# A four-layer sequence kernel: VectorE computes y first at the changes of unit, and the experts' weights and six norms are prepared in the mixer's last steps

## The reference

```
# mixer: 128 heads of 64 channels, 8 groups, state of 128; four-tap causal convolution on x, B, C
gate, xBC, dt = split(x @ in_proj_w.T);  xBC = silu(conv(xBC) + conv_b)
y = ssd(x_heads, -exp(A_log), B, C, D, softplus(dt + dt_bias))    # in chunks, with a carried state
g = y * silu(gate);  g = g * rsqrt(mean(g*g over a group's 1024 channels) + eps) * norm_w
x3 = layernorm(x2 + g @ out_w.T)
# experts: 28 of them, the two best per token
base = x3 @ base_W.T;  logits = x3 @ gate_W.T;  h = x3 @ lora_A.T (28 x 8 columns)
out = layernorm(x3 + base + (h * gates * 2) @ lora_B)
```

## Time and profile before

| | |
|---|---|
| time, median of 3 runs | 2229.35 us |
| profiled execution: time | 2232.77 us |
| profiled execution: span of instructions | 2230.7 us |
| busy: PE / PEld / DVE / ACT / POOL | 2085.4 / 1627.8 / 1717.7 / 1444.4 / 1144.1 us |
| mean granted clock of TensorE, share of full | 0.974 |

### The profile page before, as it was taken

One profiled execution on the slowest core, in us unless ns is written; L12 is line 12 of the kernel. 1 busy time (PEld: TensorE's weight loads), 2 busy tenths in 40 slices (PEclk: granted clock), 3 DMA queues, 4 the chain that ended last, 5 costly groups with the idle time before them and its releaser, 6 DMA issues. The chain is left out here.

```text
span 2230.7 us, 32403 instructions
## 1 busy us (share of the span) xinstructions
PE 2085.4 (93%) x10968; PEld 1627.8 (73%) x10968; DVE 1717.7 (77%) x2864; ACT 1444.4 (65%) x2823; POOL 1144.1 (51%) x976
## 2 busy tenths in 40 slices
PE   8899896999999999999999999999999999999968
PEld 4666575787777778777877777778777777777755
DVE  4777574878887988788778877887888788878766
ACT  1566524776777676767776778667767776777631
POOL 3554240555555564565465646564656465545531
PEclk9899997999999999999999999999999999999979
DMA  4000011312131213221322122112221212121111
GB/s 161 1 0 0 1 53 40 94 64 86 39 99 62 84 46 92 81 73 39 99 71 72 63 75 71 71 63 76 70 76 58 80 67 86 48 86 57 38 37 38
DMA packets 72194, 140.28 MB, mean 63 GB/s; under 512 B 34449, under 2 KB 35473, under 8 KB 67826
## 3 DMA queue, kind: packets, MB, share of 16 engines
q1 hardware_dynamic: 72050, 138.44, 18.6%
HBM read 134.74 MB, written 3.67 MB: 62 GB/s over the span
## 5 line engine op out<-in xcount | busy, mean ns | idle before, releaser
L92 PE MATMUL p_out<-w_out,yT 128*128 128x512 f32 x1536 | 384.4, 400 | 22.2 <-issue 14.2
L92 PE MATMUL p_mix<-x_high,w_x 128*128 128x512 f32 x1024 | 384.2, 437 | 1.4 <-DVE x_low L1028 1.4
L1680 POOL TENSOR_TENSOR wq_t<-wq_t,cb 128x1024 f32<-128x1024 f32 x128 | 326.7, 2552 | 88.2 <-DVE cb L1555 85.5
L92 PEld LDWEIGHTS p_out<-w_out,yT 128*128 128x128 f32 x1536 | 291.9, 192 | 90.9 <-issue 18.2
L764 DVE SCALAR_TENSOR_TENSOR conv<-p_mix,unit_small,conv 128x511 f32<-128x511 f32 (+2 forms) x384 | 287.0, 747 | 89.2 <-ACT conv L744 80.1
L92 PE MATMUL p_gate<-w_gate,x_high 128*128 128x512 f32 x1024 | 327.5, 401 | 0.2 <-ACT silu_gate L1406 0.2
L1398 ACT ACTIVATE wq_t<-wq_t,minus_cum 128x128 f32<-128x128 f32 x1024 | 313.9, 389 | 1.4
L1335 PEld LDWEIGHTS p_intra<-x_dt,wq_t 128*128 128x128 f32 x2048 | 241.0, 192 | 4.6 <-POOL wq_t L1680 2.2
L1335 PE MATMUL p_intra<-x_dt,wq_t 128*128 128x64 f32 x2048 | 242.8, 272 | 1.0 <-POOL wq_t L1680 1.0
L92 PEld LDWEIGHTS p_mix<-x_high,w_x 128*128 128x128 f32 x1024 | 195.3, 191 | 62.5 <-issue 22.2
L752 ACT ACTIVATE x_channels<-conv 128x512 f32<-128x512 f32 x128 | 80.8, 631 | 222.1 <-DVE conv L764 220.5
(11 more groups left out here) (228 smaller groups left out, 4248.3 us busy)
## 6 DMA issues: line engine op xcount, KB each, us to landing
cum_all<-cum_rows SPq DMA_DIRECT2D x128, 512.0 KB, 3.6
w_staged<-in_w_gate SPq DMA_DIRECT2D x16, 1024.0 KB, 6.0
w_raw_tiles<-in_w_x SPq DMA_DIRECT2D x64, 256.0 KB, 3.7
w_staged<-in_w_out SPq DMA_DIRECT2D x16, 1024.0 KB, 4.8
w_raw_tiles<-in_w_bc SPq DMA_DIRECT2D x16, 256.0 KB, 2.7
x<-in_x SPq DMA_DIRECT2D x1, 2048.0 KB, 17.4
out<-z SPq DMA_DIRECT2D x8, 256.0 KB, 2.0
wqkv<-in_wqkv SPq DMA_DIRECT2D x4, 384.0 KB, 5.4
```

What stands on the lines that cost most here:

```text
L92: last = pe.matmul(dst, left[a](k), right[b](k), start=k == 0 and n_ == 0, stop=stop and k == tiles - 1 and n_ == 2)
L1680: pool.tensor_tensor(decay[:, k % 2], decay[:, k % 2], cb[:, c].unsqueeze(1).to_broadcast([P, UNIT_HEADS, P]), ALU.mult).then_inc(decay_do ...
```

## The change

In the mixer VectorE's order is another one at the changes of unit. `make_y` is the old code of y. In the last step of a unit it stands ahead of the taps; in the first, all four low parts of `w_out` stand ahead of it and the output sum behind it. The output sum of step 14 goes to step 0 of the next group, `arguments` of step 1 and 9 behind the copies of `p_mix`, and the cast and low part of `w_bc` from step 8 to step 9 on both engines.

A class `Ahead` holds what the last group does for the experts. Their weights go to buffers of the mixer that are free by then: raw tiles to `w_staged`, `w_raw_tiles` and `conv`, loaded in step 13; high and low parts to `w_x`, `w_bc` and, for the last low part, `w_gate`; `w_lora_b` to `cum_all`, loaded in step 15. ScalarE makes the high parts at the ends of steps 14 and 15, GpSimd all four low parts there. In steps 12 to 15 VectorE takes the moments of chunks 0 and 1, 2 and 3, 4, and 5 behind y, and the norm of the chunk before; GpSimd takes their powers behind `inv_rms`. In the experts the loads, splits and first six moments fall away; `pS` lies in `p_mix`.

```diff
+class Ahead:
...
+    NORMED = {2 * CHUNKS - 4: (0, 1), 2 * CHUNKS - 3: (2, 3), 2 * CHUNKS - 2: (4,), 2 * CHUNKS - 1: (5,)}
+    def high_part(self, act, k):
+        act.wait_ge(self.in_w4[k], 16)
+        act.activation(self.high[k], self.raw[k], ACT.Copy).then_inc(self.w4_high, 1)
+    def low_part(self, pool, k, gate_done):
+        pool.wait_ge(self.w4_high, k + 1)
+        if k == KT - 1:
+            pool.wait_ge(gate_done, GROUPS * STEPS)
+        pool.tensor_tensor(self.low[k], self.raw[k], self.high[k].bitcast(F32), ALU.subtract).then_inc(self.w4_low, 1)
+    def moments(self, dve, i, src):
+        dve.bn_stats(self.stats[:, i % 2], src).then_inc(self.stats_done, 1)
+        dve.wait_ge(self.stats_done, 2 * i + 1)
+        dve.bn_aggr(self.mv[:, i], self.stats[:, i % 2]).then_inc(self.stats_done, 1)
+        dve.wait_ge(self.stats_done, 2 * i + 2)
+        dve.tensor_scalar(self.mv[:, i, 1:2], self.mv[:, i, 1:2], EPS, None, ALU.add).then_inc(self.var_done, 1)
+    def inverse(self, pool, i, neg_half):
+        pool.wait_ge(self.var_done, i + 1)
+        pool.tensor_tensor(self.rstd[:, i:i + 1], self.mv[:, i, 1:2], neg_half, ALU.pow).then_inc(self.rstd_done, 1)
+    def norm(self, dve, i, dst, sem):
+        dve.wait_ge(self.rstd_done, i + 1)
+        dve.tensor_scalar(dst, dst, self.mv[:, i, 0:1], self.rstd[:, i:i + 1], ALU.subtract, ALU.mult).then_inc(sem, 1)
...
@@ mixer, SP
+                        if last and k == 2 * CHUNKS - 3:
+                            sp.wait_ge(out_split, 2 * GROUPS * UT)
+                            sp.wait_ge(front.x_w_split, 2 * GROUPS * UT)
+                            sp.wait_ge(conv_done, PLAN.ready(g, CHUNKS + CPS - 1, ("x", UT - 1, 1)))
+                            ahead.load_weights(sp, d["w_experts"])
+                        if last and k == 2 * CHUNKS - 1:
+                            sp.wait_ge(arg_done, GROUPS * STEPS)
+                            ahead.load_lora(sp, d["w_lora_b"])
@@ mixer, ScalarE: high_part(0), (1) at the end of step 14; (2), (3) in step 15 behind the square
@@ mixer, VectorE
+                def ahead_norm(k):
+                    for i in ahead.NORMED[k]:
+                        dve.wait_ge(both_done, (GROUPS - 1) * CHUNKS + i + 1)
+                        ahead.moments(dve, i, acc[:, i])
+                        if i:
+                            ahead.norm(dve, i - 1, acc[:, i - 1], ahead.norm3)
-                        early = c > 0 and k + 1 < STEPS
-                        if early:
+                        if c > 1 and k + 1 < STEPS:
                             arguments(s + 1, k + 1)
...
+                        if c == 1:
+                            arguments(s + 1, k + 1)
...
                             y_low_part(*before)
+                        if k == 0 and not first:
+                            out_sum(g - 1, STEPS - 2)
...
+                        if c == CHUNKS - 1:
+                            make_y(g, k)
+                            taps_of(events)
+                            if last and half:
+                                ahead_norm(k)
+                            continue
+                        taps_of(events)
+                        if summed and c:
                             out_sum(*before)
...
-                        if k == CHUNKS and not last:
+                        if k == CHUNKS + 1 and not last:
                             for j in range(2):
                                 front.bc_high_part(dve, g * 5 + 6, j)
                         if c == 0:
-                            out_low_part(g * 2 + half, half, (0, 1))
+                            out_low_part(g * 2 + half, half)
...
+                        make_y(g, k)
+                        if summed and c == 0:
                             out_sum(*before)
-                        if c == 0:
-                            out_low_part(g * 2 + half, half, (2, 3))
+                        if last and k >= 2 * CHUNKS - 4:
+                            ahead_norm(k)
@@ mixer, GpSimd
                             inverse_rms(*before)
+                        if last and k >= 2 * CHUNKS - 4:
+                            for i in ahead.NORMED[k]:
+                                ahead.inverse(pool, i, neg_half[:])
+                        if last and k >= 2 * CHUNKS - 2:
+                            for i in range(2):
+                                ahead.low_part(pool, (k - 2 * CHUNKS + 2) * 2 + i, gate_done)
...
-                        if k == CHUNKS and not last:
+                        if k == CHUNKS + 1 and not last:
@@ experts, VectorE
-                for c in range(CHUNKS):
-                    moments(c, x3[:, c])
-                    if c:
-                        norm(c - 1, x3[:, c - 1], norm3)
...
+                for c in range(EARLY, CHUNKS):
+                    ahead.moments(dve, c, x3[:, c])
+                    ahead.norm(dve, c - 1, x3[:, c - 1], norm3)
+                    if c == EARLY:
+                        low(0)
+                ahead.norm(dve, CHUNKS - 1, x3[:, CHUNKS - 1], norm3)
```

More of the change, by code:

```diff
@@ L1457, in group @@
                         if c == CHUNKS - 1:
+                            if half and last:
+                                ahead.high_part(act, 2)
+                                ahead.high_part(act, 3)
                             if half and not last:
@@ L1470, in group @@
                             empty_x(g, k + 1)
+                        if last and k == 2 * CHUNKS - 2:
+                            ahead.high_part(act, 0)
+                            ahead.high_part(act, 1)
                 groups(act, group)
@@ L1478, in _, with out_low_part @@
                 dve.memset(neg_half[:], -0.5).then_inc(const3, 1)
-                def out_low_part(unit, half, tiles):
-                    for j in tiles:
+                def out_low_part(unit, half):
+                    for j in range(UT):
                         at_ = UT * (TAPS + 1) + j
@@ L1535, in out_sum, with make_y @@
                                              ALU.mult, ALU.add).then_inc(both_done, 1)
+                def make_y(g, k):
+                    s, c = step(g, k), k % CHUNKS
+                    dve.wait_ge(intra_done, s + 1)
+                    if carries(c):
+                        dve.wait_ge(skip_sum, n_carries(g, k) + 1)
+                    else:
+                        dve.wait_ge(xskip_done, s + 1)
+                    yk = y[:, k % 2]
+                    wait(dve, sq_done, s - 1)
+                    dve.tensor_tensor(yk, p_intra[:], xskip[:].rearrange("p h e -> p (h e)"),
+                                      ALU.add).then_inc(y_sum, 1)
+                    dve.wait_ge(sg_done, s + 1)
+                    dve.wait_ge(y_sum, s + 1)
+                    dve.tensor_tensor(yk, yk, sg[:], ALU.mult).then_inc(y_done, 1)
+                def ahead_norm(k):
[4 more added lines that the diff above has]
+                            ahead.norm(dve, i - 1, acc[:, i - 1], ahead.norm3)
                 def group(g, first, last):
@@ L1707, in experts @@
         n = Named(nc, ctx)
-        ident, x3 = keep["ident"], keep["acc"]
-        w = n.sb("w_experts", [P, KT, DIM + SIDE])
-        w_high = n.sb("w_experts_high", [P, KT, DIM + SIDE], F32R)
-        w_low = n.sb("w_experts_low", [P, KT, DIM + SIDE], F32R)
-        wb = n.sb("w_lora_b", [P, 2, DIM])
+        ident, x3, ahead = keep["ident"], keep["acc"], keep["ahead"]
+        w_high, w_low, wb = ahead.high, ahead.low, ahead.lora
         iota = n.sb("iota", [P, EXPERTS])
         neg_half = n.sb("neg_half4", [P, 1])
-        stats = n.sb("ln4_stats", [P, 2, nc.vector.BN_STATS_DIM])
-        mv = n.sb("ln4_mv", [P, 2 * CHUNKS, 2])
-        ve = n.sb("ln4_ve", [P, 2 * CHUNKS])
-        rstd = n.sb("ln4_rstd", [P, 2 * CHUNKS])
         xT = n.sb("x3T", [P, 2, 2, KT, P], F32R)
@@ L1807, in _ @@
                 flip(0)
-                pe.wait_ge(w4_low, 2)
-                pe.wait_ge(w4_low_pool, 2)
+                pe.wait_ge(ahead.w4_low, KT)
                 for c in range(CHUNKS + 1):
@@ L1926, in finish @@
                     dve.wait_ge(z_done, c + 1)
-                    moments(CHUNKS + c, z[:, c])
+                    ahead.moments(dve, CHUNKS + c, z[:, c])
                     if c:
-                        norm(CHUNKS + c - 1, z[:, c - 1], norm4)
+                        ahead.norm(dve, CHUNKS + c - 1, z[:, c - 1], norm4)
                 for c in range(CHUNKS + 1):
@@ L1935, in _ @@
                         finish(c - 1)
-                norm(2 * CHUNKS - 1, z[:, CHUNKS - 1], norm4)
+                ahead.norm(dve, 2 * CHUNKS - 1, z[:, CHUNKS - 1], norm4)
 def build(nc, d, out):
@@ L1965, in build @@
                 layer0_tail(nc, d, keep)
+            keep["ahead"] = Ahead(nc, Named(nc, lasting), keep["front"])
             mixer(nc, d, keep)
-        experts(nc, d, keep, out)
+            experts(nc, d, keep, out)
 def laid_out(x):
```

105 lines of the change are left out of this document (47 added, 58 removed).

## The result

The changed kernel takes 2201.47 us, median of four runs (2200.19 to 2203.4), beside 2229.09 of the kernel before on the same chip: ratio 0.9877, 95% interval 0.9864 to 0.9891, a gain of 27.6 us. Its profiled execution took 2200.28 us (span 2198.5, mean granted clock 0.979); the one before took 2232.77, so that pair differs by 32.5 us. Of the 32.5, 1.8 lie ahead of the mixer, which was not changed. Forecast: 2208, range 2194 to 2223.

What follows compares the result with a forecast made beforehand. TensorE, busy nearly all of the span, was taken as the bound, only its waits winnable. Mixer -22 us and last steps with experts +0.5 sum to -21.5, from a median of 2229.35 to 2208 us, range 2194 to 2223.

Steps and rivals of the forecast that it cites:

- Step 7 to 8: Mixer, into step 8: y directly after p_intra removes the flip's 1.02 us wait; gain 0.6 us a group.
- Step 9's flip: Mixer, flip of y in step 9: wait falls from 1.16 to 0.4 us; gain 0.8 a group.
- Output product of step 8: Mixer, in step 9: yT no longer behind low parts and arguments; gain 1.8 us a group.
- Step 10: Mixer, step 9 to 10: arriving w_bc casts and low parts make a 2.0 us wait for 0.87; loss 1.1 a group.
- Step 15 to 0: Mixer, group change: y's 1.73 us wait goes, but x's product waits for the taps; gain 0.35 us.
- The last group: Mixer's last group, without casts or next group: 0.6 - 0.4 + 1.6 + 0.5 = 2.3 us gain.
- Clock: Mixer, slow output products after the 1.80 us wait in three groups: 3 of 4.7 us regained.
- the ring from decay to decay: Last steps: dependent VectorE and GpSimd passes take 15.3, then 15.9 us, where TensorE's step takes 12; mixer's end +14 us.
- The further 1 us of clock: Experts: about 1 us more gained from a clock that is back sooner.
- the last steps keep their gain: Rival, chance 0.12: GpSimd's wait is hidden and the mixer ends as today; 2195 us.
- VectorE is the bound: Rival, chance 0.18: at the changes of unit the order only passes the wait on, gaining 8 us; 2221.
- Slower: Rival, chance 0.07: w_bc's casts and low parts in step 9 make the group wait twice; 2248 us.

Runs made afterwards that it cites:

- e8: The kernel before, with only y put ahead of the taps in the last step of a unit: 2220.91 us, ratio 0.9965.
- e1: The kernel before, with only VectorE's and GpSimd's new order at the changes of unit, experts' preparation as before: 2199.81 us, ratio 0.9872.
- e4: The changed kernel, with the two casts of w_bc in step 9 behind y instead of ahead of the state's product: 2236.14 us, ratio 1.0033.
- e9: The changed kernel, with the casts and low parts of w_bc back in step 8: 2229.88 us, ratio 1.0010.
- e3: The changed kernel, with GpSimd's powers and VectorE's norms one step later, low parts in steps 14 and 15, loads one step earlier: 2196.71 us.
- e5: The changed kernel, with moments and norms behind the mean square, powers behind inv_rms, high and low parts moved, loads in step 12: 2195.11 us.
- e10: As e5, but w_experts' low parts: none in step 13, one each in 14 and 15, two behind the last inverse of the mean square: 2193.55 us.
- e6: The changed kernel, with GpSimd's two low parts of w_bc moved behind its decay product of step 10: 2213.59 us, ratio 0.9938.
- e2: The changed kernel with VectorE's old order at the changes of unit, keeping only the experts' preparation in the last steps: 2234.93 us, ratio 1.0027.

## Why the prediction was right, and where its sizes were off

The mechanisms all came as described, and both parts had the right sign or zero. The mixer was worth more than the 22 us forecast: 30.2 in the two profiles, read between step 10's flips (4.0 up to the first, 23.7 in six intervals, 2.5 in the last). That pair lies 4.9 us further apart than the medians, so some of it is scatter; the medians say 27.6 for the 21.5 forecast in all. Term by term:

- Step 7 to 8: 0.66 measured (1.02 less 0.36) for 0.6; e8 shows it alone.
- Step 9's flip: 1.16 for 0.8. The four low parts took 3.53, y's multiply ended at 1161.88, as TensorE came (its flip starts at 1162.11). The 0.4 us of wait that I kept did not come.
- Output product of step 8: 1.80 for 1.80.
- Step 10: a wait of 1.51 for 2.0, so a loss of 0.64 and not 1.1. The mis-sized term is the casts: I took the second at 1.26, "held by the first low part". Both ran at 0.42. The rows at 1.26 were held by something else (below). The state's product took 1.79 for 1.5, as long as the longest of the earlier trace rows.
- Step 11: a wait of 0.51 that I did not look for. GpSimd's passes are 3 us later in step 10 and `x_skip` takes 2.02 beside VectorE.
- Step 15 to 0: 0.71 for 0.35. Released by the taps, as said, but y's multiply ahead of them took 1.00 and not 1.27.
- Sum: 0.66 + 1.16 + 1.80 - 0.64 - 0.51 + 0.71 = 3.2 for 2.45; the usual interval between flips says 3.4 (218.46 less 215.04), and 0.2 us have no wait of their own in the trace.
- The last group: 2.3 for 2.3, by luck. The 0.4 us of wait in step 9's flip did not come, and step 10's flip, forecast to gain 0.5, waits 0.84 as before (0.85): VectorE's passes beside GpSimd there did not change. The two errors cancel.
- Clock: 3 us forecast. The longer intervals of before held 3.5 us more than the usual one, those of after 0.3, and the first group gained 1.0 beyond its waits: 4.2.

The last steps: the ring from decay to decay was 15.2 and 15.5 us for 15.3 and 15.9. TensorE's idle time was 3.14 us ahead of the output product of step 13 (4.6 forecast) and 8.17 ahead of `p_intra` of step 15 (8). From the output product of step 11 to the mixer's end it took 63.87 instead of 51.45 us: +12.4 for +14. The 12.6 after it came exactly. The further 1 us of clock did not: from the first product to the end 67.2 us, 67.1 before. Net -0.2 for +0.5; that the net is so near is in part two errors of opposite sign.

The rival "the last steps keep their gain" was wrong by e1 and the tail, "VectorE is the bound" by step 10's 1.51 and the 27.6 us. "Slower" did not come, but e4 and e9 show how near it was: with the same casts a few passes later or one step earlier, the change would have been worth nothing or have cost a few us. I gave the casts in step 9 a chance of 0.07 to hurt, from bounds of contention; what decided was which engine started first.

## What to carry to other kernels

Before an operation is put on an in-order queue, ask what its input waits for: if it comes later than the data of the next pass in that queue, the whole wait is added to the pass (here 12.4 us given back in the last steps, and 35 us lost over seven groups by casts a few passes later, e4). An engine whose idle time is large in the sum may still have no idle place there; put such work behind an operation that waits for the same data anyway, as `inv_rms` (e3, e5, e10). And where two engines contend, a pass costs little when it begins while the other engine is waiting for it, so count starts and not only durations (e9 lost some 29 us by the same casts one step earlier).

## What the runs showed of the hardware

The casts of `w_bc`, all sixteen, VectorE's line 776 in after (minimum, median, maximum in ns), where the earlier trace rows has 415/1264/1870 for before:

```profile
L776 DVE CAST w_bc<-w_raw_tiles x16: 416/420/422, 302.8 to 1817.0; 128x512 fp32r<-128x512 f32 x16
```

Before, the pair began at 1168.46, inside GpSimd's decay product, which is followed by `x_skip`. GpSimd's timeline of before, step 8:

```profile
1167.61 2.41 POOL L1680 TENSOR_TENSOR wq_t<-wq_t,cb 128x1024 f32<-128x1024 f32 x1
```

It ends at 1170.02, `x_skip` at 1171.21 and the casts at 1171.49. After, GpSimd is idle 3.46 us up to its first low part, which waits for the first cast; the second cast starts ahead of it:

```profile
1171.76 3.12 POOL L788 TENSOR_TENSOR w_bc<-w_raw_tiles,w_bc 128x512 fp32r<-128x512 f32 x2 [3.46 <-DVE w_bc L776]
```

In e6, where `x_to_state` starts 0.1 us before them, they take 2.46. The Trainium skill, "SBUF — State Buffer", Who interferes with whom, says it in one sentence: "Issue order, not op shape, decides who blocks." The three placements agree.

Passes of two inputs follow the same order. In e4 VectorE's skip sum starts 0.15 us behind GpSimd's decay product (1194.32 and 1194.17): it takes 2.77 where it takes 0.69 alone, and the decay product keeps its 2.37. y's multiply starts 0.02 us behind `x_skip` (1203.94 and 1203.92) and takes 1.56 for 0.69, while `x_skip` keeps its 1.04. The decay product behind `x_skip` starts while that multiply still runs, and now it is GpSimd's pass that is longer, 2.80.

TensorE's granted clock and its pauses: after, it was 1.00 over 412.58 to 2064.62 with waits of 1.5 us in each group, 0.87 over 2064.62 to 2128.50. Behind 2.40 us of idle time twelve output passes took 4.62 us and behind 3.14 us 4.37, in place of 2.95, behind 8.17 us sixteen passes of `p_intra` 3.67 in place of 2.00, near the ratio of its two levels, 2.4 and 1.2 GHz, for the part of them that ran at the lower. The length of the pause alone does not decide: in e2 the same pause as the 3.14 (3.15 there) was followed by twelve passes in 3.01 us, and the 1.80 us of before by 4.4 to 4.6 us in three groups and by 3.0 in the others.
